# First edge pass of a two-layer graph network: 16 steps of gathered rows fetched during the node pass

## The reference, cut to what matters

```python
h = jnp.maximum(_layernorm(x, axis=-1), 0.0)
x = x + _L0_gnn_ref(src, dst, h, L0_gnn_W, L0_gnn_b)
...
# _L0_gnn_ref(row=src, col=dst, X=h, W, b)
deg = 1.0 + jax.ops.segment_sum(jnp.ones((E,), X.dtype), col, num_segments=N)
dinv = jax.lax.rsqrt(deg)
XW = X @ W + b
scaled = XW * dinv[:, None]
msg = jax.ops.segment_sum(scaled[col], row, num_segments=N)
out = (msg + scaled) * dinv[:, None]
```

## Time and profile before

| what | value |
|---|---|
| median of 3 runs | 2155.31 us (2149.29 to 2168.29) |
| the profiled execution | 2154.57 us, its span 2152.7 us |
| busy share of the span | PE 79%, PEld 67%, DVE 83%, ACT 71%, POOL 51% |
| mean granted TensorE clock | 0.931 |
| list pass of GpSimd | 328.97 to 708.5 us |
| first edge pass, first to last gather of x rows | 708.8 to 1023.4 us |
| its last scatter-adds and the first gather of e2 | 1051.61 and 1053.46, then 1057.47 us |

### The profile page before, as it was taken

The page is one execution under the profiler, slowest core; times in us unless marked ns, Lnnn a source line. Parts: engine busy times, 40 slices in busy tenths (PEclk is TensorE's granted clock), DMA queues, the critical chain, the costliest instruction groups (busy, mean ns, idle before and its releaser), DMA issues.

```text
span 2152.7 us, 53890 instructions
## 1 busy us (share of the span) xinstructions
PE 1692.0 (79%) x14246; PEld 1444.6 (67%) x14344; DVE 1780.1 (83%) x7827; ACT 1529.4 (71%) x3485; POOL 1095.4 (51%) x1065
## 2 busy tenths in 40 slices
PE   5979999999999798888578777679997777787100
PEld 3657888888888677777466666568885777777100
DVE  5778999999999688888488888779987999999664
ACT  3757788878788577877566666579996999999100
POOL 3105654455545577787567777744430222122576
PEclk9989999999999899999798999989998999999655
DMA  4689666666666577777456666567785888888784
GB/s 143 239 202 217 239 235 232 230 241 244 232 234 210 148 157 160 164 158 156 78 106 120 122 119 118 102 205 248 246 218 189 290 287 291 287 288 288 261 279 148
DMA packets 206640, 437.75 MB, mean 203 GB/s; under 512 B 49624, under 2 KB 87900, under 8 KB 206570
## 3 DMA queue, kind: packets, MB, share of 16 engines
q1 hardware_dynamic: 137018, 361.19, 49.2%
q0 software_dynamic: 56448, 74.95, 19.1%
q10 hardware_dynamic: 13104, 0.81, 1.5%
HBM read 220.18 MB, written 219.18 MB: 204 GB/s over the span
## 4 chain that ended last, share of the span: by engine, by line
PE 37%; issue 15%; ACT 13%; DMA 12%; POOL 10%; DVE 9%; SPq 1%; DVEq 1%; ACTq 0%; POOLq 0%
PE bank L817 15%; ACT hb L1087 7%; PE bank L797 6%; POOL big L503 4%; DMA big<-x_tab,idx 3%; DVE st L1349 2%; POOL msg_tab L514 2%; PE bank L776 2%; POOL x_tab L514 2%; DMA big<-in_x_dram,idx 2%; DMA out_dram<-osb,idx 2%; ACT ht L1236 2%; PE bank L813 2%; PE bank L938 2%; PE bank L948 2%
## 5 line engine op out<-in xcount | busy, mean ns | idle before, releaser
L1349 DVE BATCH_NORM_STATS2 st<-big 128x6 f32<-128x256 f32 x882 | 314.9, 413 | 87.8 <-DMA big<-x_tab,idx 65.4
L817 PE MATMUL bank<-w_sb,ht 128*128 128x256 f32 x1568 | 371.6, 380 | 9.8 <-issue 7.7
L817 PEld LDWEIGHTS bank<-w_sb,ht 128*128 128x128 f32 x1568 | 299.9, 191 | 47.5
L797 PE MATMUL bank<-ident,hb 128*128 128x128 f32 x1568 | 211.1, 278 | 89.6 <-ACT hb L1087 75.7
L503 POOL DMA_INDIRECT big<-x_tab,idx x196 | 193.1, 985 | 144.4 <-issue 51.9
L469 POOL DMA_INDIRECT node_edge<-node_tab,idx x196 | 188.3, 961 | 138.9 <-issue 50.6
L797 PEld LDWEIGHTS bank<-ident,hb 128*128 128x128 f32 x1568 | 178.3, 142 | 119.2 <-issue 83.6
L563 POOL TENSOR_TENSOR big<-big,bias 128x256 f32<-128x256 f32 x98 | 72.0, 734 | 324.1 <-ACT hb L1087 285.4
L1048 ACT ACTIVATE hb<-big,rs 128x256 f32<-128x256 f32 x392 | 207.5, 590 | 21.1 <-DVE rs L1372 21.1
L1087 ACT ACTIVATE hb<-big,rs 128x256 f32<-128x256 f32 x392 | 213.5, 591 | 4.0 <-DVE rs L1372 3.9
L1031 ACT ACTIVATE sd<-mv,eps_col 128x4 f32<-128x4 f32 (+1 forms) x343 | 103.2, 301 | 154.1 <-DVE mv L1358 153.8
(11 more groups left out here) (248 smaller groups left out, 4360.2 us busy)
## 6 DMA issues: line engine op xcount, KB each, us to landing
big<-in_x_dram SPq DMA_DIRECT2D x97, 512.0 KB, 4.2
x_tab<-x1b SPq DMA_DIRECT2D x97, 512.0 KB, 2.9
big<-x_tab SPq DMA_DIRECT2D x97, 512.0 KB, 4.2
out_dram<-x1b SPq DMA_DIRECT2D x97, 512.0 KB, 2.9
x_odd<-x1b SPq DMA_DIRECT2D x48, 512.0 KB
big<-x_odd SPq DMA_DIRECT2D x48, 512.0 KB
msg_tab<-zeros SPq DMA_DIRECT2D x50, 256.0 KB, 2.2
tpw_tab<-tpb SPq DMA_DIRECT2D x49, 256.0 KB, 2.0
```

The costliest lines, as they stand in the source:

```text
L797: last = nc.tensor.transpose(bank[q][:, (2 * j + k) * P:(2 * j + k + 1) * P], hb[:, s.slot(2, 2), 2 * q + j, k * P:(k + 1) * P], ident[:])
L817: last = mm(y, ht[:, q, (2 * j + k) * P:(2 * j + k + 1) * P], w_sb[:, k, :], start=False, stop=(j == 1 and k == 1))
L1349: last = v.bn_stats(st[:, k, j, :], row)
```

## The change

A buffer `shared` of 32 KB per partition is a ring `ahead` of 16 steps for x rows; the buffers that other passes need (for the MLP, for e2 and e3) now lie in it, since they are not in use at that time. GpSimd fills all 16 steps in the list pass, a pair of gathers after the list steps 5, 11, ..., 95. In e1 it gathers the rows for steps 16 to 48 alone, at the steps 4 + (k-16)*44//32, so in three of four steps, into the same ring, when ACT has used the step of 16 earlier. DVE and ACT read `ahead` in e1, and their loops have a body of 16 steps in place of 4. The semaphores e1_got and the order gather, scatter-add within a step stay.

```diff
+AHEAD = 16
...
+        shared = sb("shared", [P, AHEAD * 2 * D])
+        ahead = shared[:].rearrange("p (s a d) -> p s a d", s=AHEAD, a=2)
+        ea16_sb = shared[:, 22 * D:22 * D + T * R]
...
+            def ahead_of_e1(s):
+                landed(pool, e1_got, s, 4, dmas=2)
+                for i in range(2):
+                    t = 2 * s.k + i
+                    pool.indirect_dma_start(ahead[:, s.k, i, :], None, x, rows_of(idx3[:, 1, t:t + 1])
+                                            ).then_inc(e1_got[s.slot(0, 4)].sem, 16)
+
             def list_step(s):
...
                 of_node_step(1, t)
+                if t % 6 == 5 and t // 6 < AHEAD:
+                    ahead_of_e1(Step(0, t // 6, t // 6, S, 4))
...
             def e1_step(s):
-                if s.live():
-                    gather(e1_got, s, 1, x, lambda s: done(pool, e1["relu"], s, 4))
+                for k in range(AHEAD, S):
+                    if s.k == 4 + (k - AHEAD) * (S - 5) // (S - 1 - AHEAD):
+                        n = Step(0, k, k, S, 4)
+                        gather(e1_got, n, 1, x, lambda n: done(pool, e1["relu"], n, AHEAD), ahead[:, n.k % AHEAD])
                 if s.k == 4:
                     x1_landed(pool)
                 scatter_add(e1, e1_out, s, 4, x1_tab)
...
-            run(act, S, 3, e1_step)
+            run(act, S, 3, e1_step, first=1, unroll=AHEAD)
...
             def edge_moments(sm, got_sems, s, dmas):
+                rows = ahead[:, s.slot(0, AHEAD)] if sm is e1 else xg[:, s.slot(0, 4)]
                 landed(dve, got_sems, s, 0, dmas=dmas)
-                return moments(sm, "chain_a", 0, [xg[:, s.slot(0, 4), i, 0:D] for i in range(2)], s)
+                return moments(sm, "chain_a", 0, [rows[:, i, 0:D] for i in range(2)], s)
...
-            run(dve, S, 3, e1_step)
+            run(dve, S, 3, e1_step, first=1, unroll=AHEAD)
```

More of the change, by code:

```diff
@@ L228, in build @@
         node_edge = sb("node_edge", [P, T, 2, 3])
-        ea16_sb = sb("ea16_sb", [P, T * R])
+        shared = sb("shared", [P, AHEAD * 2 * D])
+        ahead = shared[:].rearrange("p (s a d) -> p s a d", s=AHEAD, a=2)
+        ea16_sb = shared[:, 22 * D:22 * D + T * R]
         ea4_sb = sb("ea4_sb", [P, T, 4])
@@ L239, in build @@
         rbf = sb("rbf", [P, 2, 2, C])
-        mlp_t = sb("mlp_t", [P, 4, P])
+        mlp_t = shared[:, 20 * D:22 * D].rearrange("p (l e) -> p l e", l=4)
         tpb = sb("tpb", [P, 2, 2, 4, C])
@@ L253, in build @@
         h2 = sb("h2", [P, 2, 2, ROW])
-        hw = sb("hw", [P, 2, 2, D])
+        hw = shared[:, 16 * D:20 * D].rearrange("p (s i d) -> p s i d", s=2, i=2)
         vb = sb("vb", [P, 2, 2, D])
@@ L271, in build @@
         asq = x1b[:, :, 2 * D:4 * D].rearrange("p s (k e) -> p s k e", k=4)
[L272 to L276, removed]
+        vvs = shared[:, 14 * D:15 * D].rearrange("p (s e) -> p s e", s=2)
+        scaleds = shared[:, 15 * D:16 * D].rearrange("p (s e) -> p s e", s=2)
+        term = shared[:, 12 * D:14 * D].rearrange("p (s i e) -> p s i e", s=2, i=2)
+        bsb = shared[:, 8 * D:12 * D].rearrange("p (s k e) -> p s k e", s=2, k=4)
+        osb = shared[:, 0:8 * D].rearrange("p (s i d) -> p s i d", s=2, i=2)
         g_sb = sb("g_sb", [P, 2, C + 1])
@@ L493, in list_step, with gather @@
                 of_node_step(1, t)
+                if t % 6 == 5 and t // 6 < AHEAD:
+                    ahead_of_e1(Step(0, t // 6, t // 6, S, 4))
             run_written_out(T, 0, list_step)
-            def gather(got_sems, s, which, table, free):
+            def gather(got_sems, s, which, table, free, to=None):
                 landed(pool, got_sems, s, 4, dmas=2)
                 free(s)
+                rows = xg[:, s.slot(0, 4)] if to is None else to
                 for i in range(2):
                     t = 2 * s.k + i
-                    pool.indirect_dma_start(xg[:, s.slot(0, 4), i, :], None, table, rows_of(idx3[:, which, t:t + 1])
+                    pool.indirect_dma_start(rows[:, i, :], None, table, rows_of(idx3[:, which, t:t + 1])
                                             ).then_inc(got_sems[s.slot(0, 4)].sem, 16)
@@ L1121, in e1_step @@
                     for i in range(2):
-                        last = s_act(hg[:, a, i, :], xg[:, s.slot(1, 4), i, 0:D], ACT.Relu,
+                        last = s_act(hg[:, a, i, :], ahead[:, s.slot(1, AHEAD), i, :], ACT.Relu,
                                      bias=rs[:, 0, a, 1, i:i + 1], scale=rs[:, 0, a, 0, i:i + 1])
```

## The result

The changed kernel takes 2196.51 us in the median of 4 runs (2193.68 to 2205.44), the kernel before 2155.26 in the same comparison: a ratio of 1.019, 95% interval 1.0135 to 1.0245. That is 41 us more, above the forecast's 2162 and above the range's upper end of 2180. The profiled execution has a span of 2194.8 us, 42.1 more than before.

The account below looks back on a forecast made before the run. It took the edge pass to be bound by the chain of scatter-add landings, 6.41 to 6.48 us a step. Terms: 2154.6 + 15.0 (list pass) - 4.2 (edge pass start) - 3.5 (scatter chain) = 2161.9, said as 2162; range 2144 to 2180.

Parts of the forecast that it names:

- The edge pass is bound by the scatter-adds' landings.: First edge pass: each scatter-add waits for the last one's landing, 6.41 to 6.48 us a step; gathers fill that wait.
- The start of the edge pass gives 4.2 us.: Edge pass start: DVE's waits for its first two x rows, 0.64 and 3.59 us, vanish with the ring full.
- runs behind its pace already: List pass: GpSimd waits 6.9+3.4 us for the node pass's pace, 133.3 for landings, so it can't catch up.
- The scatter chain of 314.1 us: Edge pass, first to last scatter: 32 periods at 6.59 and 16 at 6.45 us, against 317.55, a gain of 3.5.
- the slow periods: Edge pass scatter periods, such as 7.6 us, held to come from late x rows and to go with the ring's lead.
- The direct lengthening of the list pass, 25 us: List pass: 16 steps with a pair go from a mean 3.51 to 5.08 us, 16 x 1.57, some 25 us.
- What of the 25 remains I estimate ... I take 15.: List pass: waits tied to the node pass's rhythm give part back; its end moves 7 to 18 us, taken as 15.
- The ceiling of 41: Most the list pass could lengthen: 25 plus 1 us for each of 16 list scatters queued behind a pair.
- The rival on the other side: List pass: pairs' packets delay the next list scatter's landing; 26 to 41 us less 7.7, likeliest 2178 us; chance 14%.
- The range: Whole kernel, 8 in 10: 2144 to 2180 us, leaving out the issue case and the landing case's upper part.
- The issue rival: Edge pass bound by GpSimd's issue time, falling from 6.59 to 5.85 us a step; 2132 us; chance 6%.
- What the longer loop costs I put at nothing.: DVE's 16-step edge-pass loop: one jump back over 674 instructions costs nothing, or up to 4.3 us if cover is missing.

Follow-up runs that it names:

- long_loop: Kernel before with only DVE's loop of the first edge pass at 16 steps in place of 4: 2146.63 us against 2144.52, ratio 1.0003.
- early: Changed kernel with its 16 pairs moved from the list pass to ahead of the node gathers: 2155.98 us against 2144.2 for the kernel before, ratio 1.0047.

## Why the prediction was wrong, by its own steps

- **The edge pass is bound by the scatter-adds' landings.** Right, and now shown: 6.49 us without and 6.52 with gathers in the changed kernel, 6.38 to 6.41 with none at all, and there the rows stand ready some 7 us ahead of the scatter that takes them.
- **The start of the edge pass gives 4.2 us.** Right in kind, 6.0 measured; but only where the list pass ends last, which is true of the first profile of the kernel before (by 0.16 us) and not of the second. I took one profile for the kernel. That GpSimd "runs behind its pace already" is likewise true of the first and not of the second.
- **The scatter chain of 314.1 us.** Measured 319.7. The 44 ordinary periods are as forecast (6.55 in the mean), but four take 7.35 to 8.33 us, and a gain of 3.5 became a loss of 2.2. I had laid the slow periods to x rows that came late, and expected the ring's lead to take them away. That was wrong: they are there with no gather in the pass at all. And of the rows fetched in the pass, only those of step 16 lead by 12 steps; the lead shrinks to none at step 48.
- **The direct lengthening of the list pass, 25 us.** Right: 5.07 us for each of the 16 steps, 25.1 in sum.
- **"What of the 25 remains I estimate ... I take 15."** This is the step that failed. Over the pass nothing was given back, and 18 us came on top: 43.4. I had let a rhythm in a table of intervals stand for a mechanism, namely that the end of a landing is a moment set by the node pass's transfers, so that a late scatter waits less. The steps right behind a pair show the contrary, 4.32 us in the mean instead of 3.32, and with memsets in the 16 places the idle time ahead of the list scatters fell only from 154.3 to 147.2 us. I now read a landing as a latency counted from its issue, plus the traffic that it meets then. That is a reading; the traffic part was not taken apart.
- **The ceiling of 41.** The rival on the other side had the right size: all of the 25, and 1 us more for each list scatter behind a pair, 41; measured were 25.1, 16.0 in the steps behind a pair (their landings 1.04 us later) and 2.4 elsewhere. Its mechanism, the pairs' packets in the queue, is shown in part at most, since landings behind a mere pause were later too, by 0.2 and 0.9 us. What was wrong is its chance of 14%: it needed only that both parts are simply added, which was the plainest reading.
- **The range.** Its upper end of 2180 left out half of a rival whose price I had computed, on the ground that the pairs would be absorbed in part.
- **The issue rival** (2132) was rightly thought unlikely.
- **"What the longer loop costs I put at nothing."** The stall is there, 4.39 us once, at the loop of 674 instructions; the loops of before show 0.33 a turn. It isn't free. In all twelve profiles with the 16-step body the scatter period beside it takes 7.9 to 8.9 us, 8.33 in the changed kernel, and the five without have none over 6.9 us there. That is some 1.8 us of the changed kernel's 41. In `long_loop` the rows came late; in the changed kernel they stood ready 4.8 us ahead and the landing itself came late, and why a stall of DVE should do that isn't known.

What stays open: which transfers of the node pass a list scatter meets, and so why its landing has a median of 2.8 us in one execution and 3.4 in another; how the price behind a pair divides between the pause and the DMAs; and why `early`, whose list pass has no pair in it, is 0.47% above the kernel before. That its node gathers start at 188 us instead of 174 to 176, and its node pass some 2 to 4 us later, was seen; that this is the cause wasn't tried.

## What to carry to other kernels

Idle time of an engine in a chain of its own DMAs (issue, landing, next issue) isn't free room: work put between a wait and the next issue lengthened the chain here by all that went beyond the step's own interval (25 us), and nothing of it was given back later; the next step became longer too (16 us). DMAs put there cost more than a pause of the same length, 9.7 us in medians of four for those of small rows, though with overlapping intervals. Idle time behind another engine's pace was room: four pairs there cost nothing, to within 0.3%. And before a gain is computed from a wait in one profile, look at a second execution for whether the chain that makes the wait is the last one there too.

## What the runs showed that I had not expected

- The list pass takes 358.5 and 377.3 us in two profiles of the kernel before and 367.7 and 393.9 in two of `early`; the landing of its scatters in the kernel before is 2.8 or 3.4 us in the median.
- Gathers of 12-byte rows cost 34 us over the kernel before, those of 1 KB rows 41, memsets of the same length 25: an 85 times smaller row took away only 6 of the 41 us (and no more than 18, if the base of these kernels, `early`, is counted off).
- DVE's one jump back over a body of 674 instructions stalls it for 2.9 to 4.5 us in all twelve profiles that have a loop body of 16 steps, and for 0.33 with 173. The Trainium skill (Runtime: NRT & Kernel Launch, Instruction fetch mechanics) says that a jump out of the two resident blocks of 256 instructions stalls for a fetch; the trace agrees, at 4.39 us in the changed kernel.
